# One loop over token groups: later layers in pieces between the heads, value and output weights fetched pair by pair

## The chip, the cores and the metric

The kernel runs on one core of one Trainium2 chip. The metric is device time in microseconds, the median of the runs shown. PE is TensorE (matrix products and transposes), DVE is VectorE, ACT is ScalarE, POOL is GpSimd, SP is SyncE, whose queue issues nearly all transfers.

## What is computed

4096 tokens (64 sequences of 64) of 256 features pass through four layers, each added to the tokens with a gate:

```python
x = x + jnp.tanh(g_xattn[0]) * _L0_xattn_ref(_layernorm(x), ctx_2048, ...)
x = x + jnp.tanh(g_ffn[0])   * _L0_ffn_ref(_layernorm(x), ...)
x = x + jnp.tanh(g_xattn[1]) * _L1_xattn_ref(_layernorm(x), ctx_2048, ctx_2048)
x = x + jnp.tanh(g_ffn[1])   * _L1_ffn_ref(_layernorm(x), ...)
```

- Layer 1: attention of each sequence's tokens to its context, 16 heads of 128; queries and keys are RMS-normalised over all 2048 inner features, then an output projection of 2048x256. (The text branch of the reference is empty here, since a context has 64 rows.)
- Layer 2: a dense 256x256 product with bias, plus a low-rank update by the two best of 8 experts, weighted by a softmax of their two logits.
- Layer 3: sigmoid attention per sequence, `V . sigmoid(Q^T K / 8)`, where the feature axes meet: a 256x256 affinity for each sequence.
- Layer 4: the best of 8 experts of rank 64, scaled by its probability.

## The kernel before

The tokens are worked on in 8 groups (`NG`) of 512, held as 4 tiles (`NT`) of 128. Matrix operands are split into a high and a low float32r part, and `three` computes hi.hi, hi.lo and lo.hi.

**Two programs, one after the other.** `first_attention` runs layer 1 for all groups and stores each group's result to memory (`x1_scratch`); `remaining_layers` then loads it and runs layers 2 to 4. The first holds the q, k, v and output weights, hi and lo, in SBUF; that memory is given to the second's tiles afterwards. Both use all 8 PSUM banks.

**First attention.** After a preparation (weights in, split in hi and lo, two Gram matrices that give the norms of queries and keys), each group takes 16 steps, one per head `h`. On each engine the order of a step is written out by hand in `step`. On PE: `prob_transpose(h-3)`, `output(h-4)`, the key projection of head h, `attend(h-3)`, `scores(h-1)`, `values(h)`, the query projection. On DVE: `prob_copy(h-3)`, `probabilities(h-2)`, `attn_lo(h-3)`, `logits(h-1)`. On ACT: the evacuation of keys, `attn_hi(h-3)`, values, `exps(h-1)`, queries. `scores` and `prob_transpose` share bank `at_ps`: PE may transpose head h-3 in step h only when DVE has taken the logits of head h-2 in step h-1; `attend(h-3)` needs `prob_copy(h-3)`; the next group's layer norm (`tile_stats`, `tile_variances`, `tile_scales`), its transposes and its Gram sums are spread over steps 2 to 14. In step 0 DVE also makes `ct_lo`, `xt_lo` (`split`) and the factors `rr` (`score_factors`).

**Remaining layers.** A software pipeline of three stages over groups: A (layer 2) of group i, B (layer 3) of i-1, C (layer 4) of i-2. `RING` lists in what order PE works and takes the 8 banks. A layer norm is `layernorm`: 4 `bn_stats` and 18 small operations, linked one by one. `low_parts` on POOL makes the low parts of the transposed tiles. `stay_awake` puts idle products of `w0t` on PE at the beginning and end of this pipeline. The output tile is stored group by group.

Of the kernel before, what the change touches and what calls it, by code (L numbers as in the profile page):

```python
# [5 lines left out]
F32 = mybir.dt.float32  # L18
F32R = mybir.dt.float32r
# [8 lines left out]
INNER = H * HD  # L28
DC = D // P
# [29 lines left out]

# [27 lines left out]

# [6 lines left out]
def rsqrt(dve, chain, y, t, v):  # L94
    rsqrt_guess(dve, chain, y, t, v)
    rsqrt_newton(dve, chain, y, t, v, 3)


def moments(dve, chain, mean, var_eps, t, stats):

# [6 lines left out]
    chain.link(dve.tensor_scalar(var_eps, t, 1.0 / D, LN_EPS, ALU.mult, ALU.add))  # L107

# [9 lines left out]
REST = "rest"  # L118


class Shared:
# [3 lines left out]
    def __init__(self, nc, stack):  # L125
        def sb(name, shape):
            return stack.enter_context(nc.sbuf_tensor(name, shape, F32))

        def sem(name):
            return stack.enter_context(nc.semaphore(name))  # L130

        self.ident = sb("ident", [P, P])
        self.tg = sb("tg", [P, 4])
        self.bias0 = sb("bias0", [P, D])
        self.gbias = sb("gbias", [P, E0])
        self.prefer = sb("prefer", [P, NT, E0])
        self.tokens = sb("tokens", [P, NT, D])
        self.context = sb("context", [P, NT, D])
        self.xs = sb("xs", [P, DC, GT])
        self.cs = sb("cs", [P, DC, GT])  # L140
        self.gram = sb("gram", [P, 2, DC, D + 1])
        self.gram_j = sb("gram_j", [P, 2, D])
        self.xres = sb("xres", [P, NT, D])
        self.s_raw = sem("s_raw_rest")
        self.rstd = sb("rstd", [P, NT])
        self.shift = sb("shift", [P, NT])
        self.scales = Signal(sem("scales_rest"), 1)
        self.x1_out = Signal(sem("x1_out"), 16)
        self.x1_in = Signal(sem("x1_in"), 16)
        self.cin_in = Signal(sem("cin_in_rest"), 16)  # L150


def raw_weights(shared):

    cs = shared.cs[:, :, :].rearrange("p c n -> p (c n)")
    return (cs[:, 0:DC * D].rearrange("p (c d) -> p c d", c=DC),
            cs[:, DC * D:DC * D + D],
            cs[:, DC * D + D:DC * D + 2 * D].rearrange("p (o e r) -> p o e r", o=2, e=E0),
            shared.xs[:, :, :].rearrange("p c n -> p (c n)").rearrange("p (c d) -> p c d", d=D),
            shared.gram[:, :, :, :].rearrange("p n c d -> p (n c d)")[:, 0:2 * E1 * R1].rearrange(  # L160
                "p (o e r) -> p o e r", o=2, e=E1),
            shared.gram_j[0:E0, :, :])


def first_attention(nc, shared, late, x, ctx, g_xattn, g_ffn, b0, gate_b,
                    q_w, q_b, ki_w, ki_b, vi_w, vi_b, o_w, o_b, nq_s, nki_s, x1_dram):


    CHAIN_PER = 100
    PREP_USES = 2 + 2 * 10  # L170
    PREP_BANKS = 6
    RAW_SLOTS = 3
    BSQ_READY = 2
    ATT_LAG, OUT_LAG = 3, 4
    LN_STEP, TR_STEP, GRAM_STEP = 6, 8, 9
    x_t = x.rearrange("b s d -> (b s) d").rearrange("(g t p) d -> g p t d", g=NG, p=P)
    c_t = ctx.rearrange("b s d -> (b s) d").rearrange("(g t p) d -> g p t d", g=NG, p=P)
    with ExitStack() as stack:
        def sb(name, shape, dt=F32):
            return stack.enter_context(nc.sbuf_tensor(name, shape, dt))  # L180

        def sem(name):
            return stack.enter_context(nc.semaphore(name))

        def signal(name, per):
            return Signal(sem(name), per)


        w_hi = {n: sb(f"{n}_hi", [P, DC, INNER], F32R) for n in "qkv"}
        w_lo = {n: sb(f"{n}_lo", [P, DC, INNER], F32R) for n in "qkv"}  # L190
        wo_hi = sb("wo_hi", [P, H, D], F32R)
        wo_lo = sb("wo_lo", [P, H, D], F32R)

        gram = shared.gram
        bsq = sb("bsq", [P, 2, H])
        beta = sb("beta", [P, 2])
        ident, xin, cin, xs, cs, xres, tg = (shared.ident, shared.tokens, shared.context, shared.xs, shared.cs,
                                             shared.xres, shared.tg)
        ones = sb("ones", [P, P])
# [1425 lines left out]
```

## Time and profile before

| | |
|---|---|
| Time, median of 3 runs (lowest to highest) | 1524.62 us (1524.61 to 1529.27) |
| Span of the profiled execution | 1542.4 us |
| PE busy | 1444.9 us, 94% |
| PE weight loads busy | 1272.6 us, 83% |
| DVE busy | 963.7 us, 62% |
| ACT busy | 639.9 us, 41% |
| POOL busy | 151.4 us, 10% |
| HBM traffic | 31.26 MB read, 8.39 MB written, 26 GB/s |

Busy times are those of one profiled execution, which took 17.8 us longer from first to last instruction than the median run. A matmul's end is modelled, so what PE really takes for a piece of work is read from the distance between starts.

### The profile page before, as it was taken

To read this page: it belongs to the slowest core of one execution; us is meant where nothing else is said; L and a number is where in the kernel's file an instruction comes from. 1 tells how busy PE (TensorE), PEld (TensorE's weight loads), DVE (VectorE), ACT (ScalarE), POOL (GpSimd) and SP (SyncE) were. 2 spreads that over 40 slices of the span, in tenths; PEclk is the share of its full clock that TensorE was granted. 3 is DMA by queue.
4 is the path that set the end of the run, shared out by engine and by line. 5 is a ranking of instruction groups with operands and counts; after the bars stand their busy time and mean duration, and the time that the engine had idled before them with its cause. 6 is when DMAs were issued, how large, how long until landed. Compare 5 with 4: busy or idle time off the path is not lost. (4 is left out here: it accounts for less than half of the span.)

```text
span 1542.4 us, 28883 instructions
## 1 busy us (share of the span) xinstructions
PE 1444.9 (94%) x10731; PEld 1272.6 (83%) x10731; DVE 963.7 (62%) x2915; ACT 639.9 (41%) x1125; POOL 151.4 (10%) x112
## 2 busy tenths in 40 slices
PE   6799999999999999999999999999778898889887
PEld 5689889989988988998898899888666777668766
DVE  6555665666576566657657666656667766685543
ACT  3334444344343443434434443444334344443442
POOL 3100000000000000000000000000112332232231
PEclk9999999999999999999999999999887887777787
DMA  5300000000000000000000000020000000100000
GB/s 181 114 2 1 29 28 2 28 2 28 16 15 28 1 29 28 1 28 2 28 1 29 28 1 1 25 73 1 28 28 28 29 28 27 41 27 14 27 15 28
DMA packets 32111, 41.30 MB, mean 27 GB/s; under 512 B 5473, under 2 KB 28993, under 8 KB 31361
## 3 DMA queue, kind: packets, MB, share of 16 engines
q1 hardware_dynamic: 31808, 39.38, 7.6%
q8 instruction: 91, 1.49, 0.4%
q0 software_dynamic: 192, 0.27, 0.1%
q14 instruction: 20, 0.16, 0.0%
HBM read 31.26 MB, written 8.39 MB: 26 GB/s over the span
## 5 line engine op out<-in xcount | busy, mean ns | idle before, releaser
L834 DVE SCALAR_TENSOR_TENSOR ao_lo<-bank,vecs,ao_hi 128x512 fp32r<-128x512 f32 x128 | 96.2, 751 | 227.7 <-ACT ao_hi L472 227.5
L827 DVE COPY pt<-bank 64x128 f32<-64x128 f32 x512 | 147.4, 288 | 127.3 <-PE bank L614 121.4
L483 ACT ACTIVATE k_sb<-bank,vecs 128x512 f32<-128x512 f32 x128 | 88.1, 688 | 260.7 <-PE bank L539 260.7
L487 ACT ACTIVATE v_sb<-bank 128x512 f32<-128x512 f32 x128 | 76.5, 598 | 233.4 <-PE bank L539 233.4
L539 PE MATMUL bank<-wo_hi,ao_hi 128*128 128x256 f32 x512 | 155.2, 303 | 2.7 <-DVE ao_lo L834 2.7
L539 PE MATMUL bank<-v_hi,ct_hi 128*128 128x256 f32 x512 | 156.3, 305 | 0.0
L539 PE MATMUL bank<-wo_hi,ao_lo 128*128 128x256 f32 x512 | 144.7, 283 | 0.0
L539 PE MATMUL bank<-wo_lo,ao_hi 128*128 128x256 f32 x512 | 144.6, 282 | 0.0
L539 PE MATMUL bank<-v_hi,ct_lo 128*128 128x256 f32 x512 | 144.4, 282 | 0.0
L539 PE MATMUL bank<-v_lo,ct_hi 128*128 128x256 f32 x512 | 144.3, 282 | 0.0
L623 PEld LDWEIGHTS bank<-pt,v_sb 128*128 128x128 f32 x1024 | 133.3, 191 | 13.2 <-issue 2.8
L623 PE MATMUL bank<-pt,v_sb 128*128 128x128 f32 x1024 | 136.8, 276 | 0.9 <-issue 0.4
L490 ACT ACTIVATE q_sb<-bank,qbias,qscale 128x512 f32<-128x512 f32 x128 | 99.5, 777 | 58.5 <-PE bank L539 58.5
L425 POOL TENSOR_TENSOR xres<-xres,obias 128x1024 f32<-128x1024 f32 x8 | 19.2, 2397 | 931.9 <-DMA xres<-in_x_dram 931.9
L472 ACT ACTIVATE ao_hi<-bank,vecs 128x512 fp32r<-128x512 f32 x128 | 87.9, 687 | 43.6 <-PE bank L623 43.6
L539 PE MATMUL bank<-ct_hi,k_hi 128*128 128x512 f32 x256 | 102.4, 400 | 3.0 <-DVE ct_lo L818 3.0
L1354 PE MATMUL ban2k<-context,xn 64*128 64x256 f32 x256 | 66.5, 552 | 41.2 <-DVE result L1536 33.3
L539 PEld LDWEIGHTS bank<-v_hi,ct_hi 128*128 128x128 f32 x512 | 96.6, 189 | 6.7 <-issue 0.2
L539 PE MATMUL bank<-xt_hi,q_hi 128*128 128x512 f32 x256 | 101.8, 398 | 0.0
L539 PE MATMUL bank<-xt_lo,q_hi 128*128 128x512 f32 x256 | 101.6, 397 | 0.0
L539 PE MATMUL bank<-ct_lo,k_hi 128*128 128x512 f32 x256 | 101.6, 397 | 0.0
L539 PE MATMUL bank<-xt_hi,q_lo 128*128 128x512 f32 x256 | 100.5, 392 | 0.0
(243 smaller groups left out, 3476.5 us busy)
## 6 DMA issues: line engine op xcount, KB each, us to landing
context<-in_ctx_dram SPq DMA_DIRECT2D x16, 512.0 KB, 4.8
tokens<-in_x_dram SPq DMA_DIRECT2D x8, 512.0 KB, 4.1
xres<-in_x_dram SPq DMA_DIRECT2D x8, 512.0 KB, 3.9
x_scratch<-xres SPq DMA_DIRECT2D x8, 512.0 KB, 2.6
tokens<-x_scratch SPq DMA_DIRECT2D x8, 512.0 KB, 3.3
out_dram<-result SPq DMA_DIRECT2D x8, 512.0 KB, 2.9
raw<-in_L_xattn_ki_w_dram SPq DMA_DIRECT2D x2, 1024.0 KB, 8.1
raw<-in_L_xattn_vi_w_dram SPq DMA_DIRECT2D x2, 1024.0 KB, 5.8
```

Source lines behind the costliest of these rows:

```text
L425: pool.tensor_tensor(xres[:, :, :], xres[:, :, :], obias[:, :].unsqueeze(1).to_broadcast([P, NT, D]), ALU.add).then_inc(xres_ready.sem, 1)
L472: act.activation(ao_hi[:, :], pv_ps[:, :], ACT.Identity, bias=vecs[:, 4 * H + h % H:4 * H + h % H + 1]).then_inc(ao_hi_ready.sem, 1)
L483: act.activation(k_sb[:, h % 2, :], bank[:, :], ACT.Identity, bias=vecs[:, 3 * H + h:3 * H + h + 1]).then_inc(pj_read.sem, 1)
L487: act.activation(v_sb[:, (h // 2) % 2, t:t + 2, :], bank[:, :].rearrange("p (t n) -> p t n", t=2), ACT.Copy).then_inc(pj_read.sem, 1)
L490: act.activation(q_sb[:, :], bank[:, :], ACT.Identity, scale=qscale[:, h:h + 1], bias=qbias[:, h:h + 1]).then_inc(pj_read.sem, 1)
L539: last = pe.matmul(out, lhs[a], rhs[b], start=start and n == 0, stop=stop and n == 2, **kw)
L623: last = pe.matmul(pv_ps[:, t * P:(t + 1) * P], v_sb[:, (h // 2) % 2, t, (h % 2) * HD:(h % 2 + 1) * HD], pt[:, t, :], start=True, stop=True)
L827: last = dve.tensor_copy(pt[b * SEQ:(b + 1) * SEQ, q::2, b * SEQ:(b + 1) * SEQ], src[:, :, b * SEQ:(b + 1) * SEQ])
L834: dve.scalar_tensor_tensor(out=ao_lo[:, :], in0=pv_ps[:, :], scalar=vecs[:, v:v + 1], in1=ao_hi[:, :].bitcast(F32), op0=ALU.add, op1=ALU.s ...
L1354: last = pe.matmul(b[:, c * D:(c + 1) * D], xn2[rows, t, c * P:(c + 1) * P], cin[rows, t, :], start=True, stop=True)
```

## The change

Both programs become one (`layers`). The loop body b works on layer 1 of group b and, between its heads, on layers 2 to 4 of group s = b-1 and on the preparation of group n = b+1. A step has five points, "a" to "e", at which the function `share` of each engine may place a piece: a is before the key projection, b after it, c before `values`, d after it, e after the query projection. I write (4,c) for step 4, point c. Body 0 has no later layers; body 8 (`NG`) has only them. Bodies 2 to 6 are a hardware loop.

```diff
+        def share(b, h, p):           # on ACT, cut
+            n, s, parts, at = b + 1, b - 1, parts_of(b), (h, p)
+            if "N" in parts:
+                if at == (1, "c"):
+                    normalise(n)
...
+            if "S" in parts:
+                if at == (4, "c"):
+                    later_normalise(s, 0, xres, xn1_ready)
+                if at == (4, "e"):
+                    turned(s, "xt1", 0, xt1_full, x2t[0], xt1_hi_ready)
+                if at == (8, "a"):
+                    later_normalise(s, 1, x2, xn2_ready)
+                if at == (11, "b"):
+                    later_normalise(s, 2, x2, xn3_ready)
...
-    w_hi = {n: sb(f"{n}_hi", [P, DC, INNER], F32R) for n in "qkv"}
+    w_hi = {n: sb(f"{n}_hi", [P, DC, INNER], F32R) for n in "qk"}
+    sv = sb("sv", [P, 2, 2, DC, 2 * HD], F32R)
+    so = sb("so", [P, 2, 2, 2, D], F32R)
...
+    o_ps, pj_ps, at_ps, pv_ps, side = banks[0:2], banks[2:4], banks[4], banks[5], banks[6:8]
...
+        def fetch_values(b, p, h):
+            sp.wait_ge(pj_full.sem, pj_full.count(b, 3 * h + 1))
+            sp.dma_start(pair(sv, p), v_dram[p]).then_inc(sv_in[p % 2].sem, 16)
...
+        def body(b):                  # on SP
+            if not is_body(b, NG - 1):
+                load_inputs(b + 1)
+            for h in range(1, H, 2):
+                fetch_outputs(b, (h - 1) // 2)
+                if h + 3 < H:
+                    fetch_values(b, (h + 3) // 2, h)
+                elif not is_body(b, NG - 1):
+                    if h == H - 1:
+                        store(b - 1)
+                    fetch_values(b, (h + 3 - H) // 2, h)
+                if h == 7:
+                    load_residual(b)
+                if h == 9:
+                    load_context(b)
...
-            pool.tensor_tensor(lo, feature_major(whole, j), hi.bitcast(F32), ALU.subtract).then_inc(ready.sem, 1)
+        def turned_low(s, name, j, hi_ready, ready):      # now on DVE
+            dve.tensor_tensor(lo, token_major(bank_of(name, j)), hi.bitcast(F32), ALU.subtract).then_inc(ready.sem, 1)
```

What moves and what changes, in full:

- **Pieces of the later layers** (S), by point: DVE statistics of x1 (3,d) to (4,a); normalised (4,c); turned (4,e), (5,a); expert rows `xa` (5,c), (5,d); choice (5,e); gates (6,b), (6,d); layer 2 product (7,a), (7,b); statistics (7,c) to (7,e); context turned (7,d), (7,e); normalised (8,a); context sum (8,b); 8 affinities (8,c) to (9,e); attention (10,a), (10,c); statistics (10,d) to (11,a); normalised (11,b); turned (11,d), (11,e); logits (12,b), (12,c); layer 4 from (12,e) to (15,b).
- **Pieces of the next group** (N): its statistics stand at (0,e), (1,a), (1,b) instead of steps 2 to 7, ACT's `normalise` at (1,c) instead of step 7, four transposes from (1,e) to (2,c) instead of steps 8 to 11, the Gram products from (2,d) to (3,b). Their count is unchanged.
- **PSUM**: all side pieces share two banks, `side`; the order of use is one list, and a piece waits until the bank's former content is read (`take`).
- **Weights**: values and outputs are split into hi and lo during body 0, one pair of heads per two steps, and kept in memory (`v_scratch`, `o_scratch`); from then on each pair (512 KB for values, 512 KB for outputs) is fetched anew in each body, into one of two buffers. Preparation waits for the q and k splits only. The small weights of layers 2 to 4 are loaded and turned in steps 12 to 15 of body 0.
- **POOL** keeps three operations of 128x1024 per body: the output bias, the bias of layer 2, the context sum. All low parts go to DVE, which reads the PSUM bank itself; ACT's float32 copies of the turned tiles fall away, except the context's.
- x1 stays in SBUF: no `x1_scratch`, no reload. `stay_awake` is gone.

In the hardware loop, on DVE, from the factors `rr` of step 0 to `ao_lo` of step 1. Before (`L811` `score_factors`, `L827` `prob_copy`, `L853` `probabilities`, `L834` `attn_lo`):

```order
L811 TENSOR_SCALAR rr<-bank,rqk 64x64 x8
L827 COPY pt<-bank 64x2x64 x4
L851 TENSOR_REDUCE rsum<-expo 128x4
...
L853 TENSOR_TENSOR prob<-expo,rinv 128x256
L834 SCALAR_TENSOR_TENSOR ao_lo<-bank,vecs,ao_hi 128x512
```

After:

```order
L1284 TENSOR_SCALAR rr<-bank,rqk 64x64 x8
...
L1242 BN_STATS stats<-xin 128x6 x4
L1299 COPY pt<-bank 64x2x64 x4
L1323 TENSOR_REDUCE rsum<-expo 128x4
...
L1325 TENSOR_TENSOR prob<-expo,rinv 128x256
L83 TENSOR_TENSOR mean<-stats 128x4
...
L89 TENSOR_SCALAR var_eps<-nt_t 128x4
...
L1251 SCALAR_TENSOR_TENSOR shift<-mean,rstd 128x4
L1306 SCALAR_TENSOR_TENSOR ao_lo<-bank,vecs,ao_hi 128x512
```

The four statistics now stand ahead of `prob_copy` of step 1, and the whole chain of the layer norm between `probabilities` and `attn_lo`.

On ACT, step 1 of the loop, where `xin` is normalised for the next group. Before (L483 keys, L472 `attn_hi`, L487 values, L477 exponentials):

```order
L483 ACTIVATE k_sb<-bank,vecs 128x512
...
L472 ACTIVATE ao_hi<-bank,vecs 128x512
...
L487 ACTIVATE v_sb<-bank 128x512
...
L477 ACTIVATE expo<-logit 128x256
...
L490 ACTIVATE q_sb<-bank,qbias,qscale 128x512
```

After:

```order
L644 ACTIVATE k_sb<-bank,vecs 128x512
...
L633 ACTIVATE ao_hi<-bank,vecs 128x512
...
L611 ACTIVATE xin<-xin,shift,rstd 128x256 x4
...
L648 ACTIVATE v_sb<-bank 128x512
...
L638 ACTIVATE expo<-logit 128x256
...
L651 ACTIVATE q_sb<-bank,qbias,qscale 128x512
L616 ISA
L618 ACTIVATE xs<-bank 128x2x128
```

The normalisation, which waits for DVE's `shift`, stands ahead of the evacuation of the values and of everything behind it.

## Rows read from the trace of the kernel before

**Rows 1.** The page: the clock granted to PE in 40 slices, in tenths.
```profile
PEclk9999999999999999999999999999887887777787
```
**Rows 2.** Stretches: from:to length, busy PE, PEld, DVE, ACT, POOL, clock, DMA.
```profile
57.11:1087.03 1029.92, 1024.17 (x8211) 914.56 (x8212) 643.80 (x1927) 434.00 (x733) 19.17 (x8) 1.00 0.06 19
1087.03:1104.47 17.44, 10.98 (x95) 9.84 (x93) 10.25 (x26) 3.26 (x5) 0.00 (x0) 1.00 0.00 1
1104.47:1542.40 437.93, 371.09 (x2200) 313.23 (x2200) 274.62 (x893) 179.83 (x363) 114.15 (x80) 0.81 0.08 28
```
**Rows 3.** The same columns: step 0 of a group, and a plain step.
```profile
445.59:453.81 8.22, 8.13 (x63) 7.00 (x64) 7.45 (x18) 3.98 (x6) 0.00 (x0) 1.00 0.01 4
461.37:468.93 7.56, 7.56 (x64) 6.80 (x63) 4.44 (x12) 3.09 (x5) 0.00 (x0) 1.00 0.01 2
```
**Rows 4.** DVE and PE in order of time in those two steps: start, length, line.
```profile
452.59 2.36 DVE L811 TENSOR_SCALAR rr<-bank,rqk 64x64 f32<-64x64 f32 x8
...
461.77 1.19 DVE L827 COPY pt<-bank 64x128 f32<-64x128 f32 x4 [1.12 <-PE bank L614]
...
463.66 0.42 DVE L853 TENSOR_TENSOR prob<-expo,rinv 128x256 f32<-128x256 f32 x1
...
464.40 1.05 PE L623 MATMUL bank<-pt,v_sb 128*128 128x128 f32 x8
...
466.21 0.75 DVE L834 SCALAR_TENSOR_TENSOR ao_lo<-bank,vecs,ao_hi 128x512 fp32r<-128x512 f32 x1 [2.12 <-ACT ao_hi L472]
...
467.78 0.42 DVE L845 TENSOR_TENSOR logit<-logit,rmax 128x256 f32<-128x256 f32 x1
```
**Rows 5.** Stretches of later layers, PE only: length, busy, clock, DMA.
```profile
1244.94:1268.64 23.70, 23.60 (x184) 1.00 0.12 41
1244.94:1247.67 2.73, 2.73 (x21) 1.00 0.44 156
1131.49:1133.15 1.66, 1.66 (x18) 1.00 0.00 0
1148.91:1150.95 2.04, 2.04 (x18) 1.00 0.00 0
1114.97:1115.42 0.45, 0.45 (x5) 1.00 0.00 0
```
**Rows 6.** Stretches on DVE: a layer norm, its end, a choice of experts.
```profile
22.81:27.60 4.79, 4.24 (x25) 1.00 0.76 284
25.66:27.60 1.94, 1.63 (x11) 1.00 1.05 443
1285.55:1288.24 2.69, 2.24 (x12) 0.50 0.00 0
```
**Rows 7.** A stretch on ACT: four tiles normalised.
```profile
1508.77:1510.89 2.12, 2.07 (x4) 1.00 0.02 4
```
**Rows 8.** POOL and DVE in order of time, where they meet.
```profile
615.97 2.39 POOL L425 TENSOR_TENSOR xres<-xres,obias 128x1024 f32<-128x1024 f32 x1 [129.84 <-DMA xres<-in_x_dram]
...
617.02 1.62 DVE L853 TENSOR_TENSOR prob<-expo,rinv 128x256 f32<-128x256 f32 x1
```
**Rows 9.** PE after two waits, and the clock behind the second (all engines).
```profile
1092.75 0.41 PE L614 MATMUL bank<-ident,prob 128*128 128x128 f32 x2 [2.28 <-DVE logit L845]
...
1276.83 2.73 PE L1354 MATMUL ban2k<-context,xn 64*128 64x256 f32 x8 [5.94 <-DVE result L1536]
...
1284.00:1288.00 4.00, 4.00 (x15) 3.04 (x15) 2.60 (x15) 1.01 (x3) 0.00 (x0) 0.50 0.00 0
```
**Rows 10.** The start of the first group's heads, DVE and PE.
```profile
52.28 2.29 DVE L316 TENSOR_TENSOR wo_lo<-raw,wo_hi 128x2048 fp32r<-128x2048 f32 x1
...
57.11 0.53 PE L539 MATMUL bank<-ct_hi,k_hi 128*128 128x512 f32 x1 [3.05 <-DVE ct_lo L818]
```
**Rows 11.** The last DVE operation, and a transfer: issues, size, us to landing.
```profile
1538.34 0.75 DVE L1536 SCALAR_TENSOR_TENSOR result<-ban2k,tg,result 128x512 f32<-128x512 f32 x1 [2.06 <-PE ban2k L1281]
...
tokens<-in_x_dram SPq DMA_DIRECT2D x8, 512.0 KB, 4.1
```

More of the change, by code:

```diff
@@ L107, in moments, with is_body @@
     chain.link(dve.tensor_scalar(var_eps, t, 1.0 / D, LN_EPS, ALU.mult, ALU.add))
+def is_body(b, n):
+    return isinstance(b, int) and b == n
 def identity(pool, sem, ident):
@@ L117 @@
 IDENT_READY = 2
[L118 to L150, printed above, removed]
@@ L165, in first_attention, with three @@
[L165 to L175, printed above, removed]
+BSQ_READY = 2
+PREP_USES = 2 + 2 * 10
+PREP_BANKS = 6
+ATT_LAG, OUT_LAG = 3, 4
+POINTS = "abcde"
+DVE_LOWS, POOL_LOWS = (0, 3), (1, 2)
+def three(pe, out, lhs, rhs, start, stop, **kw):
+    for n, (a, b) in enumerate(((0, 0), (0, 1), (1, 0))):
+        last = pe.matmul(out, lhs[a], rhs[b], start=start and n == 0, stop=stop and n == 2, **kw)
+    return last
@@ new lines, in layers @@
+    sv = sb("sv", [P, 2, 2, DC, 2 * HD], F32R)
+    so = sb("so", [P, 2, 2, 2, D], F32R)
+    xin = sb("xin", [P, NT, D])
+    cin = sb("cin", [P, NT, D])
+    xs = sb("xs", [P, DC, GT])
+    cs = sb("cs", [P, DC, GT])
+    xres = sb("xres", [P, NT, D])
+    stats = sb("stats", [P, NT, 6])
+    mean = sb("mean", [P, NT])
+    var_eps = sb("var_eps", [P, NT])
+    rstd = sb("rstd", [P, NT])
+    shift = sb("shift", [P, NT])
+    nt_t = sb("nt_t", [P, NT])
+    sums = sb("sums", [P, 2 * NT])
+    sums_b = sb("sums_b", [P, 2 * NT])
@@ new lines, in layers @@
+    rqk = sb("rqk", [P, 2 * NT])
+    nqk_t = sb("nqk_t", [P, 2 * NT])
+    rmax = sb("rmax", [P, NT])
+    rsum = sb("rsum", [P, NT])
+    rinv = sb("rinv", [P, NT])
+    with ExitStack() as early:
+        raw = [early.enter_context(nc.sbuf_tensor(f"raw{i}", [P, INNER], F32)) for i in range(4)]
+    xt_hi, xt_lo = both("xt", [P, DC, GT])
+    ct_hi, ct_lo = both("ct", [P, DC, GT])
+    v_sb = sb("v_sb", [P, 2, NT, 2 * HD])
+    k_sb = sb("k_sb", [P, 2, GT])
+    q_sb = sb("q_sb", [P, GT])
+    logit = sb("logit", [P, NT, SEQ])
@@ new lines, in layers @@
+    pick = [sb(f"pick{i}", [P, NT, E0]) for i in range(2)]
+    top = sb("top", [P, 2, NT])
+    best = sb("best", [P, NT])
+    gexp = sb("gexp", [P, NT])
+    gw = sb("gw", [P, 2, NT])
+    gates = sb("gates", [P, NT, E0])
+    csum = sb("csum", [P, NT])
+    lg1 = sb("lg1", [P, NT, E1])
+    ex1 = sb("ex1", [P, NT, E1])
+    coef = sb("coef", [P, NT, E1])
+    banks = [stack.enter_context(nc.psum_tensor(f"bank{i}", [P, 512], F32)) for i in range(8)]
+    o_ps, pj_ps, at_ps, pv_ps, side = banks[0:2], banks[2:4], banks[4], banks[5], banks[6:8]
@@ new lines, in layers, with parts_of, bank_of, token_major @@
+    PLACE = {(name, i): u for u, (name, i, _, _) in enumerate(SIDE)}
+    assert len(SIDE) % 2 == 0
+    GROUP = {"N": 1, "S": -1, "W": 0}
+    def parts_of(b):
+        if not isinstance(b, int) or 0 < b < NG - 1:
+            return "SN"
+        return {-1: "N", 0: "NW", NG - 1: "S", NG: "S"}.get(b, "")
+    def bank_of(name, i):
+        return side[PLACE[name, i] % 2]
+    def token_major(bank):
+        return bank[:, :].rearrange("p (t c n) -> p t c n", t=2, c=DC)
+    def feature_major(buf, i):
+        return buf[:, :, 2 * i * P:2 * (i + 1) * P].rearrange("p c (t n) -> p t c n", t=2)
```

2516 lines of the change are left out of this document (1274 added, 1242 removed).

## The prediction

> **What bounds the kernel now.** I read the page's clock line first: PE has its full clock for three quarters of the span and less in the last quarter [rows 1]. The stretches say why [rows 2]. From the first head's first product to the last group's last one, 1029.9 us, PE is busy for 1024.2 at clock 1.00, and no wait of weight stands there: PE is the bound and everything else hides behind it. Then 17.4 us of drain (the last heads' outputs), then 437.9 us for the later layers, with PE busy for 371.1 at a mean clock of 0.81. That last stretch is what the change is about. Its waits are serial chains: layer norm on DVE, normalising on ACT, transposing on PE. A wait of 2.28 us left the next products at full speed, but after one of 5.94 us PE ran at 0.50, its 1.2 GHz level, and was still there 7 us later, busy without a break [rows 9]. So the later layers pay twice, by idling and by the clock after it.
>
> Next, a plain step of one head. It takes 7.56 us, all of it PE, while DVE is busy for 4.4 and ACT for 3.1 [rows 3]. That leaves room on DVE for side work, but the order matters. In the plain step [rows 4] `prob_copy` runs from 0.4 to 1.6 and `attend` starts at 3.05, so the copy may be 1.4 us late. The last operation of the logits ends at 6.8 and the next step starts at 7.56, so it may be 0.7 us late, plus what PE does for side pieces behind `scores`. Step 0 has more on DVE: 8.22 us long [rows 3], and DVE's `rr` ends 9.4 us after the step began [rows 4], which the next step still absorbs.
>
> **The later layers on PE, at full clock.** A stretch of 23.70 us without a real gap holds three of the four expert tiles `h`, half of the gate logits, `xg`, the layer 2 product, `hm`, `att`, `y` and 16 transposes [rows 5]. The missing tile with the missing half of the logits is the row of 2.73. Eight more transposes are half of 1.66. The affinities are twice 2.04 (16 of 32 records each). `xa` has 24 products; four starts lie in 0.45, so 2.7. Sum 34.0 per group. Cut into some 34 pieces, each first product follows another kind; the rows do not price that alone. I bound it by 0.5 us (the long stretch holds seven kinds and shows 0.1 us idle) and 11 us (step 0, in which two pieces stand in another order, is 0.66 us longer than a plain one [rows 3]) and take 2, near the low end, since the stretch is PE work of the very kinds that move and step 0 also waits for the splits. So **36 us** per group that must go between the heads. It hides nothing on PE: PE was full, and stays full. What the change can save is the idling and the slow clock: 437.9 us become 8 x 36 = 288 at most, less what comes back as waits.
>
> **What comes back as waits in a body.** DVE's side work is about 36 us per group too: three layer norms of 4.79 [rows 6], choices and gates about 8, some sixteen 128x512 operations at 0.7 (with the eight low parts that leave POOL), the context sum. Against it stand 36 us more PE time and 16 steps x 3.1 us of free DVE. On average it fits; locally it does not. I walked the body step by step with the row values:
> - Step 1: DVE is free at 9.4. The statistics (2.85 for statistics and variances [rows 6], half of it here) bring it to 10.8, the copy to 12.0, while PE wants `attend` at 8.2 + 3.05 = 11.3. PE waits **0.8**. Then `probabilities` to 13.1, variances and scales (1.4 + 1.94) to 16.5, and ACT's `normalise` 2.1 [rows 7] to 18.6. PE stands at (1,e) from 16.6 and waits **2.0** for the first transpose. Queued behind `normalise` on ACT are the values' evacuation, the exponentials and the queries; PE needs them later than 18.6, so no more is added.
> - Step 4: after the two residuals of step 3, DVE does 2.85 at (3,d), (3,e) and enters step 4 3.4 us late; copy to 4.7, `attend` wanted at 3.05: **1.6**. Scales and ACT's normalising end at 9.9, PE is at (4,e) from 9.2: **0.6**.
> - Step 5: `square_norms` and the low part of `xt1` stand ahead of the copy: **1.4**. Step 6, behind the choice of 2.69 [rows 6]: **0.3**.
> - Step 8: the whole layer norm (7,c) to (7,e), 4.79, starts when the logits of step 7 are done: **1.3**. Queued behind it are the copy and, on ACT, the keys' evacuation behind `later_normalise` (8,a).
> - Steps 11 and 12: on ACT the normalising at (11,b) stands ahead of `attn_hi`; the transposes wait **1.2**, the next step **0.3** for the logits.
> - Steps 9, 10, 13 to 15: PE has 3 to 5 us of side work each and DVE at most 2: nothing.
>
> Sum **9.5 us** per body for bodies 1 to 6, some 5 for body 7, which prepares no next group.
>
> **Moved at no price.** ACT loses six copies per group and stays under half busy. The next group's transposes and Gram products are the same. Each body fetches 16 transfers of 512 KB for the weights and five others, some 10.7 MB in all in 165 to 180 us; one lands in 4.1 us [rows 11], while each has two to three steps, 15 us or more, between the wait that frees its buffer and its use. SP's queue is in order: `load_residual` stands behind `fetch_values` of step 7 and so starts only after that step's `values`; it has until POOL's bias, and that until the next body. If this cover were gone, each late fetch would cost its lateness in full; I see none.
>
> **Preparation.** The first product waits for DVE, which made `wo_lo` (2.29) in between [rows 10]; that goes to body 0. What is late next are the Gram sums, which now pass through one bank at a time. I take 1.4 us, between 0 and 3. Body 0 pays the 2.0 at (1,e), 28 transposes of late weights at 0.1 and a little: 6.
>
> **The end.** Body 8 has no heads to hide behind, and no second group to overlap: 17.4 drain; three layer norms with normalising 3 x 6.9 = 20.7; PE's 34 us, partly at 1.2 GHz after long waits [rows 9], 48; hi and low parts 5; choices and gates 7; residuals 2; 4 for waits on the two banks; from the last DVE operation to the end 3.3 [rows 11]. Sum **108**, between 100 and 118.
>
> **Sum.** Start 55.7, heads 1029.9, later layers 7 x 36 = 252, waits 6 x 9.5 + 5 = 62, body 0 6, end 108: **1514 us** of span against 1542.4, so 28 less. The median run stands 17.8 below the profiled span; the same difference off 1524.6 gives **1497**. I predict 1498.
>
> **POOL, and a rule on it.** POOL's bias ran from 615.97 to 618.36; `prob`, which starts at 617.02 and reads two SBUF tiles, took 1.62 instead of 0.42 and ended 0.3 after POOL [rows 8]. So DVE stands still for such operations. Three of them per body, 6.7 us. In my walk the one at 51 to 54 us falls where DVE would wait for ACT anyway and costs 1.2 (counted in step 5); the output bias lands just behind the layer norm of step 7; the third falls where there is slack. The Trainium skill, page "SBUF — State Buffer", section "Who interferes with whom", says more: whichever engine starts first holds the shared ports for its whole instruction and the other blocks fully, and copies and scalar operations in a two-port mode are hit too. By that the small operations of `square_norms` and of the layer norm would all be stopped. The row agrees for two SBUF inputs; no row here shows the scalar ones, so the sum goes by the walk.
>
> **Rivals.**
> 1. *Forecast* (50%): waits of 7 to 12 us per body: 1482 to 1514.
> 2. *More hides than I see* (12%): DVE and ACT run ahead in steps 9 to 15 and the late steps recover; waits of 2 to 6: 7 x 5 less, 1460 to 1482.
> 3. *DVE falls behind, slower* (22%): the residual load lands early or late, POOL's bias meets the layer norm of (7,c) to (7,e), 2.4 us more in front of `prob_copy`, and the other two POOL operations cost 1.5 each instead of 1.2 and 0; each piece cut off by a wait on another engine costs 0.1 more. With 4 to 8 us more per body it decides: break-even lies at 28 / 7 = 4 us more. Price: 1525 to 1550. For it: every wait in the walk is DVE's; the walk has no reserve for handovers. Against: before, step 0 took up 2.4 us of `rr` and the splits at 0.66 us of PE's time. This is where the page's rule would put it: 6.7 us of lost DVE, 5.5 more than counted, give 1498 + 7 x 5.5 = 1536.
> 4. *The clock falls in each body* (8%): my longest wait is 2.0 us, and 2.28 did no harm [rows 9]; but two waits close together might. Work of some 16 us at half clock costs 8: 7 x 8 more, 1554.
> 5. *No net change* (8%): between 1 and 3, 1514 to 1530.
>
> The overlap itself cannot fail to happen; the order on PE is written out. Faster by over 0.3% (a measurement of this kernel can't tell less from no change) is below 1520: cases 1 and 2 and part of 5, 66%. Within 0.3%: 8%. Slower: 26%. Leaving out the top of case 2 and the ends of 3 and 4, the range is 1470 to 1545.
>
> **What would show it.** Profile after: clock 1.00 until the last body; bodies of 175 us (distance between POOL's output biases), 165 with rival 2, 180 with 3; waits on PE before `attend` on `prob_copy`'s DVE line at steps 1, 4, 5, 8 and before `transposes` on ACT's `xin`; PE waits of some 62 us before the end; from the last query product to the end 108. Wrong would be: waits on DMA, a clock below 1.00 inside the bodies, or waits in steps 9, 10 or 13 to 15.

## The result and the profile after

The changed kernel takes **1546.22 us** (1544.57 to 1554.43, 6 runs) against 1530.20 (1524.61 to 1535.20, 6 runs) for the kernel before beside it: ratio 1.0104, interval 1.0067 to 1.0141, so slower by 1.0%. I had forecast 1498, and the range to 1545 ends just below it.

The page of the kernel after:

```profile
span 1542.8 us, 28633 instructions
PE 1419.3 (92%) x10671; PEld 1224.8 (79%) x10671; DVE 976.3 (63%) x3000; ACT 599.5 (39%) x1065; POOL 63.8 (4%) x42
PEclk9999999999999999999999999999999999999858
HBM read 85.78 MB, written 12.58 MB: 64 GB/s over the span
```

The overlap does what it was made for: PE's clock line is full until the last three slices, where before it fell in the last quarter [rows 1], and PE is busy for 26 us less. Yet the span is the same, 1542.8 against 1542.4. To see where the gain went I cut the span at POOL's output bias, which comes once per body (start, length):

```profile
635.20 2.35 POOL L556 TENSOR_TENSOR xres<-xres,obias 128x1024 f32<-128x1024 f32 x1 [34.48 <-DMA xres<-in_x_dram]
...
815.76 2.35 POOL L556 TENSOR_TENSOR xres<-xres,obias 128x1024 f32<-128x1024 f32 x1 [34.64 <-DMA xres<-in_x_dram]
```

The stretches between, and the whole of the heads and of the end (from:to, length, then busy time and count of PE, PE's weight loads, DVE, ACT, POOL, the granted clock, the DMA share, GB/s):

```profile
635.20:815.76 180.56, 171.39 (x1306) 147.58 (x1306) 117.47 (x368) 72.30 (x130) 6.62 (x3) 0.99 0.18 62
815.76:997.24 181.48, 171.42 (x1306) 147.66 (x1306) 117.70 (x369) 72.22 (x130) 6.63 (x4) 0.99 0.18 62
...
49.31:1434.43 1385.12, 1317.34 (x10089) 1137.57 (x10089) 901.71 (x2786) 561.80 (x1003) 48.91 (x22) 0.99 0.19 65
1434.43:1542.80 108.37, 64.74 (x358) 53.67 (x356) 44.15 (x148) 21.59 (x40) 4.24 (x2) 0.73 0.02 5
```

The end takes 108.4 us; I had forecast 108. A body takes 181; I had forecast 175. In the first stretch shown PE is not busy for 180.56 - 171.39 = 9.2 us; I had forecast 9.5 of waits. So the sum of the waits was right, and PE's *busy* time is some 6 us too long. PE's waits in that body (total, times, longest) and some of them in order of time, in brackets the idle time ahead and its releaser:

```profile
PE bank L897 <- DVE pt L1299: 4.9, 4, 1.5
PE bank L961 <- ACT xn L657: 1.5, 2, 1.1
PE bank L888 <- issue: 0.9, 1, 0.9
PE bank L908 <- issue: 0.8, 1, 0.8
PE bank L864 <- ACT xin L611: 0.7, 1, 0.7
```

```profile
593.23 1.16 PE L897 MATMUL bank<-pt,v_sb 128*128 128x128 f32 x8 [1.49 <-DVE pt L1299]
...
603.73 1.16 PE L897 MATMUL bank<-pt,v_sb 128*128 128x128 f32 x8 [1.24 <-DVE pt L1299]
...
636.42 1.16 PE L897 MATMUL bank<-pt,v_sb 128*128 128x128 f32 x8 [1.34 <-DVE pt L1299]
...
676.90 0.66 PE L961 MATMUL bank<-ident,xn 128*128 128x128 f32 x4 [1.14 <-ACT xn L657]
```

These are `attend` of steps 4, 5 and 8 and the turning at (11,d): 1.49, 1.24, 1.34 and 1.14 where the walk had 1.6, 1.4, 1.3 and 1.2. Three things were not in the walk.

**The affinities.** PE in order of time in step 8, one affinity and the product behind it:

```profile
638.12 1.13 PE L999 MATMUL bank<-cin,xn 64*128 64x256 f32 x4
639.18 0.50 PE L116 MATMUL bank<-sv,ct_hi 128*128 128x256 f32 x2
```

The next product starts 1.06 after it, and so behind the others. Eight such pieces are 8.5 us. Before, 16 records (four affinities) lay in 2.04, so eight in 4.1 [rows 5]. An affinity uses 64 of PE's 128 rows; before, one sequence's product could stand beside the next one's on the other rows, and now each has a piece for itself.

**The clock.** PE in body 2, the first pass of the hardware loop, with the two waits of step 1, and stretches behind them:

```profile
377.14 1.16 PE L897 MATMUL bank<-pt,v_sb 128*128 128x128 f32 x8 [0.99 <-DVE pt L1299]
...
383.84 0.41 PE L864 MATMUL bank<-ident,xin 128*128 128x128 f32 x2 [1.92 <-ACT xin L611]
```

```profile
382.00:384.00 2.00, 0.16 (x2) 0.19 (x3) 1.43 (x4) 2.00 (x6) 0.00 (x0) 1.00 0.56 223
384.00:386.00 2.00, 2.00 (x13) 2.00 (x13) 1.03 (x4) 1.57 (x5) 0.00 (x0) 0.59 0.04 8
386.00:388.00 2.00, 2.00 (x12) 2.00 (x12) 1.14 (x4) 0.00 (x0) 0.00 (x0) 0.56 0.00 0
388.00:390.00 2.00, 2.00 (x14) 1.69 (x14) 0.00 (x0) 1.13 (x3) 0.00 (x0) 1.00 0.00 0
```

Both waits have the forecast size (0.8 and 2.0), but behind them PE runs at its 1.2 GHz level for 3.4 us, which loses 1.7. A single wait of 2.28 had done no harm [rows 9]. Each of bodies 2 to 6 has one such stretch. Body 1 has none, although its waits in step 1 are nearly the same and as close together (for the second the profile names no releaser here):

```profile
199.11 1.16 PE L897 MATMUL bank<-pt,v_sb 128*128 128x128 f32 x8 [1.18 <-DVE pt L1299]
...
205.65 0.41 PE L864 MATMUL bank<-ident,xin 128*128 128x128 f32 x2 [1.74 <-issue]
```

```profile
206.00:208.00 2.00, 2.00 (x20) 2.00 (x19) 1.40 (x5) 1.54 (x5) 0.00 (x0) 1.00 0.00 0
```

**Waits without a releaser.** In step 0 of bodies 3 to 6, that is each time behind a jump back of the hardware loop, PE stands twice for nothing that the profile shows, 1.8 to 2.8 us in sum. Bodies 1, 2 and 7, which no jump back precedes, have no such gaps. In body 5:

```profile
907.55 0.43 PE L888 MATMUL bank<-ident,prob 128*128 128x128 f32 x2 [0.88 <-issue]
...
913.52 0.70 PE L908 MATMUL bank<-k_sb,q_sb 128*64 128x64 f32 x8 [1.95 <-issue]
```

### The profile page after: what moved, and what is told of

The parts are those of the page before. It is cut to its first block, busy times and chain, and to the rows that moved or that the text cites. A ratio compares the mean times of both kernels' runs of the same rounds, so it can differ in the third digit from the quotient of the medians.

```text
span 1542.8 us, 28633 instructions
## 1 busy us (share of the span) xinstructions
PE 1419.3 (92%) x10671; PEld 1224.8 (79%) x10671; DVE 976.3 (63%) x3000; ACT 599.5 (39%) x1065; POOL 63.8 (4%) x42
## 4 chain that ended last, share of the span: by engine, by line
PE 67%; DVE 21%; issue 6%; ACT 4%; DMA 0%; SPq 0%; DVEq 0%; ACTq 0%
PE bank L116 44%; PE bank L897 7%; PE bank L999 4%; PE bank L908 3%; PE bank L874 3%; DVE pt L1299 3%; DVE stats L1341 2%; PE bank L888 2%; ACT ao_hi L633 2%; ACT xn L657 1%; DVE rmax L1316 1%; PE bank L1011 1%; PE bank L864 1%; DVE logit L1314 1%; DVE ao_lo L1306 1%
## 5 line engine op out<-in xcount | busy, mean ns | idle before, releaser
L116 PE MATMUL bank<-so,ao_hi 128*128 128x256 f32 x1024 | 198.0, 292 | 2.9 <-DVE ao_lo L1306 2.9
L116 PE MATMUL bank<-sv,ct_hi 128*128 128x256 f32 x1024 | 197.8, 292 | 0.0
L897 PEld LDWEIGHTS bank<-pt,v_sb 128*128 128x128 f32 x1024 | 127.3, 191 | 52.3 <-DVE pt L1299 41.6
L116 PEld LDWEIGHTS bank<-sv,ct_hi 128*128 128x128 f32 x1024 | 156.2, 189 | 12.8 <-issue 7.8
L116 PEld LDWEIGHTS bank<-so,ao_hi 128*128 128x128 f32 x1024 | 156.5, 190 | 3.3 <-issue 3.3
L116 PE MATMUL bank<-so,ao_lo 128*128 128x256 f32 x512 | 143.6, 280 | 0.0
L116 PE MATMUL bank<-sv,ct_lo 128*128 128x256 f32 x512 | 142.9, 279 | 0.0
L116 PE MATMUL bank<-ct_hi,k_lo 128*128 128x512 f32 x256 | 102.9, 402 | 0.0
L116 PEld LDWEIGHTS bank<-so,ao_lo 128*128 128x128 f32 x512 | 96.8, 189 | 0.0
L116 PEld LDWEIGHTS bank<-sv,ct_lo 128*128 128x128 f32 x512 | 96.3, 188 | 0.0
```

Source lines behind the costliest of these rows:

```text
L116: last = pe.matmul(out, lhs[a], rhs[b], start=start and n == 0, stop=stop and n == 2, **kw)
L897: last = pe.matmul(pv_ps[:, t * P:(t + 1) * P], v_sb[:, (h // 2) % 2, t, (h % 2) * HD:(h % 2 + 1) * HD], pt[:, t, :], start=True, stop=True)
```

## The experiments

Times are medians of 4 or 5 runs (10 in the repeat of the kernel before); ratios are to the kernel before on the same chip, 1530 to 1534 us. Experiments 1 to 4 ran on one chip, 5 to 7 on a second, 8 and 9 on a third and 10 on a fourth, so a difference between two of these sets is good to a few us only.

**1. Affinities in pairs.** The changed kernel with

```diff
-            for c in range(DC):
-                last = pe.matmul(dst[:, c * D:(c + 1) * D], xn[rows, t, ...], cin2[rows, t, :], ...)
-            last.then_inc(aff_full.sem, 1)
+            for c in range(DC):
+                for i in range(2):
+                    rows = slice(i * SEQ, (i + 1) * SEQ)
+                    last = pe.matmul(dst[i][:, c * D:(c + 1) * D], xn[rows, t, ...], cin2[rows, t, :], ...)
+    PAIR_AT = {(8, "c"): 0, (8, "e"): 1, (9, "b"): 2, (9, "d"): 3}
```

> The changed kernel with one edit: the eight affinities of a group are issued as four pairs, each pair with the two sequences of one tile (rows 0 to 63 and 64 to 127), product by product in turn into the two side banks, at (8,c), (8,e), (9,b) and (9,d). Theory A (the affinities were priced from a stretch where two of them ran at the same time on the two halves of PE's rows; cut into single pieces they no longer overlap): each pair takes 1.0 to 1.1 us instead of 2 x 1.06, PE's affinity time per body falls from 8.5 to about 4.2, bodies from 181 to 177, and the whole from 1546 to about 1515. Theory B (the bodies are long because of DVE, of the waits it causes, or of the cuts as such): PE's saved time turns into waits on prob_copy, bodies stay at 180 or lose at most the four cuts, 1 us, and the time stays above 1538.

1519.64 us, ratio 0.9919 (0.9889 to 0.9948): 27 us less than the changed kernel. PE's piece in the trace, now two affinities:

```profile
635.24 1.13 PE L1001 MATMUL bank<-cin,xn 64*128 64x256 f32 x8
```

Twice the records in the same 1.13. Theory A's size was 31 less. Two things gave part of it back. One is POOL (experiment 5). The other is the end: from the last query product it takes 112.9 us instead of 108.8, and there each pair behind the first waits for ACT, which empties the banks:

```profile
1470.44 2.08 PE L1001 MATMUL bank<-cin,xn 64*128 64x256 f32 x8 [1.23 <-ACT th L682]
```

**2. The control.** The same with `rows = slice(0, SEQ)` for both.

> Control for the run with pairs: the same four pairs at the same places, but both products of a pair read rows 0 to 63, so the odd sequences get the affinity of the even ones (that part of the output is not the reference's). Theory A (overlap on different rows): a pair takes 2.0 us or more, as two single ones, and the time stays within 5 us of the changed kernel, 1538 to 1546. Rival (what the pairs save is four cuts between kinds of products): this run is as fast as the pairs, about 1515.

1544.49 us, 1.0088 (1.0063 to 1.0112), the time of the changed kernel. A pair now takes 1.99:

```profile
643.96 1.99 PE L1001 MATMUL bank<-cin,xn 64*128 64x256 f32 x8
```

So it is the two halves of the rows that give the gain, and not the four cuts fewer: the next product starts 1.92 behind such a pair, against 2 x 1.06 for two single pieces. The Trainium skill, page "TensorEngine Tiling (Array Packing)", section "Tiling Modes", says that tiles of the array can load weights and multiply in parallel; these rows agree.

**3. PE's loop written out.** The changed kernel with `for b in range(2, NG - 1)` in place of PE's hardware loop.

> The changed kernel with one edit: PE's hardware loop over bodies 2 to 6 is written out; the other engines keep theirs. In the trace PE idles in step 0 of each pass for nothing that is recorded (0.94 before the transposes, 0.84 to 1.9 in the middle of scores), and PE then runs some 3.4 us at its 1.2 GHz level. Theory C (the jump back of PE's loop costs this): these gaps go, 2.3 us per pass, and with them the slow stretch, 1.7 us per pass; 5 passes, so 1546 becomes 1526 to 1538. Rival (the gaps are waits on another engine or on the splits of the tokens): they stay, and the time with them.

1549.72 us, 1.0154 (1.0106 to 1.0201): nothing gained. But the gaps moved. PE's two are gone, and in the same bodies 3 to 6 DVE has one (in body 5, DVE, then PE):

```profile
907.21 1.20 DVE L1299 COPY pt<-bank 64x128 f32<-64x128 f32 x4 [4.01 <-issue]
...
908.46 1.90 PE L897 MATMUL bank<-pt,v_sb 128*128 128x128 f32 x8 [1.91 <-DVE pt L1299]
```

PE's transposes for this copy started at 904.75, 2.5 before it; in the changed kernel the copy starts 1.2 behind them. So DVE was 1.3 late on its own account, behind the jump of its own loop. Theory C's forecast failed; its mechanism may be incomplete rather than wrong: experiments 6 and 10 go on from here.

**4. Fetches made small.** The changed kernel with `pair(sv, p)[:, 0:16]` and `v_dram[p][:, 0:16]`, the same for the outputs. The index cuts columns, not partitions as I wrote: each fetch moves 16 columns of all 128 partitions, 8 KB.

> The changed kernel, but each fetch of a pair of value or output weights moves 16 of 128 partition rows (64 KB instead of 512 KB); nearly all heads then use stale weights, so the output is not the reference's. Theory D (the transfers are hidden, as forecast): within 3 us of the changed kernel. Rival (10 MB per body of writes into SBUF slow the engines' own accesses or delay instruction loading): bodies of 181 become 178 or less, time below 1530.

1571.20 us, 1.0262 (1.0236 to 1.0287): *slower* by 25 us than the changed kernel, as neither theory had it. The residual lands 3.8 us from its issue instead of 5.0 (the page's issues), behind smaller transfers in SP's queue, and so POOL's output bias starts sooner, in six of seven bodies inside the layer norm of (7,c) to (7,e). In the worst of them, POOL and DVE in order of time, PE's next wait, and the clock behind it:

```profile
1005.80 2.35 POOL L556 TENSOR_TENSOR xres<-xres,obias 128x1024 f32<-128x1024 f32 x1 [33.57 <-DMA xres<-in_x_dram]
1005.82 2.35 DVE L77 TENSOR_TENSOR ntmp<-rstd 128x4 f32<-128x4 f32 x1
1008.20 0.16 DVE L78 SCALAR_TENSOR_TENSOR ntmp<-ntmp,var_eps 128x4 f32<-128x4 f32 x1
...
1010.13 2.07 PE L897 MATMUL bank<-pt,v_sb 128*128 128x128 f32 x8 [3.53 <-DVE pt L1299]
```

```profile
1010.00:1015.00 5.00, 4.87 (x28) 3.88 (x28) 4.39 (x10) 2.12 (x4) 1.89 (x1) 0.50 0.00 0
1015.00:1020.00 5.00, 5.00 (x17) 3.80 (x16) 0.00 (x0) 1.19 (x2) 0.00 (x0) 0.50 0.00 0
```

An operation on 128x4 takes 2.35 instead of 0.16, just as long as POOL's; `attend` waits 3.5 instead of 1.3; and PE then runs at 1.2 GHz for over 10 us. That is rival 3's meeting and rival 4's clock, one setting off the other. In the changed kernel the bias starts behind the layer norm in all seven bodies, but by less than a microsecond; at 815.76 it is 0.35 us behind the end of the last operation:

```profile
815.25 0.16 DVE L1350 SCALAR_TENSOR_TENSOR shift<-mean,rstd 128x4 f32<-128x4 f32 x1
```

It escapes by luck.

**5. POOL's operations moved, and made small.** Both on top of the pairs. In the pairs run the gain of PE had moved the bias into the layer norm in four of seven bodies:

```profile
625.95 2.34 POOL L557 TENSOR_TENSOR xres<-xres,obias 128x1024 f32<-128x1024 f32 x1 [34.13 <-DMA xres<-in_x_dram]
626.02 2.29 DVE L1353 SCALAR_TENSOR_TENSOR shift<-mean,rstd 128x4 f32<-128x4 f32 x1
...
629.47 1.16 PE L898 MATMUL bank<-pt,v_sb 128*128 128x128 f32 x8 [3.26 <-DVE pt L1302]
```

```diff
+            pool.wait_ge(l_ready.sem, l_ready.count(b, 8))      # output bias, now behind the context sum
+            pool.wait_ge(l_ready.sem, l_ready.count(s + 1, 5))  # bias of layer 2
+            pool.wait_ge(l_ready.sem, l_ready.count(s + 1, 7))  # context sum
```

> The kernel with paired affinities (1519.6 us), with POOL's three operations moved: each also waits until DVE has finished the logits of a certain step (bias of layer 2: step 6, context sum: step 8, output bias: step 9, behind the context sum), so that it starts where DVE would idle. In the pairs run POOL's output bias started inside the layer norm of (7,c) to (7,e) in four of seven bodies: an operation of 128x4 that takes 0.16 took 2.3, and attend waited 3.2 instead of 1.1 to 1.3. Theory E (POOL's operation stops DVE's): attend of step 8 waits 1.3 in every body, 4 x 2 us less and a little at steps 5 and 9: 1505 to 1513. Rival (the waits come from the order on DVE itself): within 3 us of 1519.6.

1507.01 us, 0.9852 (0.9795 to 0.9908). The second kernel, on one column per tile:

> The kernel with paired affinities, with POOL's three operations per body cut to one column of each tile (128x4 instead of 128x1024): the output bias, the bias of layer 2 and the context sum are left out of all other columns. Theory E: the full price of POOL beside DVE, 4 x 2 us for the met layer norms and up to 1 us in other places of each body: 1502 to 1512, and the kernel with timed POOL operations not slower than this by more than 4 us. Rival: within 3 us of 1519.6.

1505.33 us, 0.9837 (0.9780 to 0.9895). POOL's meetings with DVE cost some 13 us in the pairs kernel, and a wait of POOL's for the right moment gives all but 2 of it back. The body between the biases is 174.83 long here, at clock 1.00. The Trainium skill, page "SBUF — State Buffer", section "Who interferes with whom", says that a DVE instruction with two SBUF inputs contends with a GpSimd instruction that reads SBUF, and that whichever issues first keeps the shared ports for its whole instruction while the other blocks fully; the rows of 2.35 and 2.29 agree. That side of the rule I had left out of the sum.

**6. All loops written out**, on top of the pairs, POOL not yet timed.

> The kernel with paired affinities (1519.6 us), with the hardware loops of all five engines written out. With PE's loop alone written out, PE's two unrecorded gaps of step 0 went, but DVE then stood for 4.0 us ahead of prob_copy for nothing that is recorded, and attend waited 1.9 for it; bodies kept their length. Theory C2 (each engine pays about 1 us at its own jump back, and they stand in line): with all loops written out both kinds of gap go, some 3 us per pass and the slow clock behind them, 5 passes: 1500 to 1507. Rival (something else in step 0 holds PE, such as the splits): the waits return under another name and the time stays at 1515 to 1523.

1510.79 us, 0.9846 (0.9780 to 0.9912); the median lies between C2's range (1500 to 1507) and the rival's (1515 to 1523), and the four runs between 1500 and 1514, too wide to tell C2's size. PE's gaps without a releaser in step 0 are gone, and so is DVE's: `attend` of step 0 starts without a wait.

**7. DVE retimed, at the wrong places.** On top of the timed POOL:

```diff
-                if at == (4, "d"):
+                if at == (9, "c"):
                     square_norms(n)
-                if at == (5, "b"):
+                if at == (9, "e"):
                     norm_factors()
-                if at == (3, "e"):
+                if at == (4, "a"):
                     later_variances()
```

and the turning of `xt3` from (11,d), (11,e) to (11,e), (12,a) on PE, ACT and DVE.

> The kernel with paired affinities and timed POOL operations, with three moves on DVE besides: square_norms and norm_factors from (4,d), (5,b) to (9,c), (9,e); the variances of the first later layer norm from (3,e) to (4,a); and the turning of xt3 one point later on all engines, (11,e) and (12,a). Theory F (the waits of attend at steps 4 and 5, 1.5 and 1.2 us, and of the transposes at (11,d), 1.1 us, are DVE work standing ahead of prob_copy or of the scales): each goes to under 0.4, some 3 us per body, 7 x 3 = 21: 1486 to 1496. Rival (DVE has no slack there, the work only moves the wait to the next step's transposes): 1500 to 1512.

1512.07 us, 0.9872 (0.9817 to 0.9928): 5 *more* than without. Theory F falls in this form. ACT and PE in order of time around step 11:

```profile
657.45 2.08 ACT L664 ACTIVATE xn<-x,shift,rstd 128x256 f32<-128x256 f32 x4 [1.43 <-DVE shift L1359]
...
662.19 0.44 PE L895 MATMUL bank<-ident,prob 128*128 128x128 f32 x2 [1.95 <-DVE logit L1326]
```

The waits of steps 4, 5 and 11 went, but ACT's normalising still stood ahead of `attn_hi`, so that `attn_lo`, the logits and the transposes of step 12 were late by what had been hidden under the old wait; `later_variances` behind the copy only moved 1.5 us to (4,e), where the transposes now waited 1.8; and `square_norms` at (9,c) met the output bias (2.58 for two operations of 128x4). The clock fell twice per body. A wait that is taken away uncovers the next one in the same chain.

**8. DVE's work moved into idle time.** Timed POOL, all loops written out, and instead of those moves:

```diff
                     residual(s, "lora", 0, lora_full, tg[:, 2:3], xres, x2_ready)
+                    dve.wait_ge(x2_ready.sem, x2_ready.count(s, 0))
+                    later_stats(x2, (0, 1))
...
+                if at == (3, "a"):
+                    first_residual(s, 0)
+                    dve.wait_ge(x1_ready.sem, x1_ready.count(s, 0))
+                    later_stats(xres, (0, 1))
+                if at == (3, "b"):
+                    first_residual(s, 1)
```

with `square_norms` at (9,a) and `norm_factors` at (14,e).

> Paired affinities, timed POOL operations (these two together 1507.0 us) and all hardware loops written out, and on DVE: the statistics of two tiles taken behind the first of the two residuals instead of all four behind the second, in step 7 and in step 3 (there both residuals move to (3,a) and (3,b), into idle time of 1.6 and 0.7 us); square_norms to (9,a) and norm_factors to (14,e). Theory H (waits fall when the work moves into DVE's idle time rather than behind another chain): attend's waits of 1.3 to 1.5 at steps 4, 5 and 8 go to under 0.3 each, 4 us per body; the loops give another 1 to 2 per pass as they did beside the pairs: 1470 to 1482. Rival (as in the retimed kernel, each wait comes back one step on): 1495 to 1505.

1466.33 us, 0.9559 (0.9513 to 0.9606): 4 us better than the low end of theory H. Of the 41 us below the kernel with timed POOL, 14 are the loops' if they cost here what they cost in experiment 10, and 27 are then left for DVE's moves, 4 per body as forecast. In the next step ACT and PE follow:

```diff
-                if at == (11, "b"):
+                if at == (11, "c"):
                     later_normalise(s, 2, x2, xn3_ready)
-                if at == (1, "e"):
+                if at == (2, "a"):
                     transposes(b, 0)
```

and `xt3` turned at (11,e), (12,a).

> The same, and the third layer norm's normalising on ACT from (11,b) to (11,c), behind attn_hi, with the turning of xt3 at (11,e) and (12,a); the next group's first transposes from (1,e) to (2,a), together with the second. Theory H: the waits of 1.1 at (11,d) and 1.9 at (1,e) go, up to 3 us per body, and with the one at (1,e) the slow clock behind it: 1450 to 1468. Rival (the retimed kernel's new waits were not ACT's order): a wait of about 1.9 before the probabilities' transposes of step 12 as there, and no gain over the kernel with split statistics.

1453.05 us, 0.9468 (0.9422 to 0.9513): 5.3% faster than the kernel before. One body between the biases, and all that PE waits for in it:

```profile
617.73:784.29 166.56, 163.61 (x1310) 143.96 (x1306) 114.62 (x367) 71.97 (x129) 6.68 (x4) 1.00 0.20 67
```

```profile
PE bank L894 <- DVE logit L1324: 1.7, 1, 1.7
PE bank L903 <- DVE pt L1306: 1.2, 1, 1.2
```

Both are left in steps 1 and 2, behind the next group's layer norm. The wait that I feared for step 12 didn't come: with the normalising behind `attn_hi` there is none.

**9. The kernel before, once more.**

> The kernel before, unchanged, profiled once more. My forecast took the profiled execution of before (1542.4 us of span, 17.8 above the median run) for a constant difference between a profiled span and a timed run. In the changed kernel the time stood 1.7 above the span in every run. Theory G (the span of the kernel before varies with the clock of its later layers, and the profile on record was a long one): this profile's span again lies 1.5 to 2 below its own run's time, that time is between 1523 and 1541, and the difference to 1542.4 lies behind 1087 us, in the later layers. Rival (profiling itself adds 18 us to this kernel): the span is 1540 or more while the timed runs are at 1530.

1532.51 us (1527.14 to 1538.55), ratio to itself 0.9988 (0.9962 to 1.0014). The profiled execution took 1531.84 with a span of 1530.0. Its last stretch, beside that of the profile on record:

```profile
1104.50:1530.00 425.50, 359.80 (x2197) 302.89 (x2195) 273.81 (x892) 178.62 (x362) 113.24 (x80) 0.83 0.08 28
```

```profile
1104.50:1542.40 437.90, 371.09 (x2200) 313.23 (x2200) 274.62 (x893) 179.83 (x363) 114.15 (x80) 0.81 0.08 28
```

All of the 12.4 us lies in the later layers, and 11.3 of it is PE's busy time at another mean clock. Theory G holds: the span lies 1.8 below its own run's time, and the span of this kernel varies with its clock. The spans of all its runs beside the experiments lie between 1521.7 and 1539.6, so that the 1542.4 on record was a long execution even so; its own time is not known.

**10. The loops back.** The 1453 us kernel with all five hardware loops.

> The fastest kernel (1453.05 us, all loops written out) with the hardware loops of all five engines back, nothing else changed. Theory C2 (a jump back costs PE two gaps that are not recorded, of about 1 us each, in step 0 of each pass, and the 1.2 GHz level behind them): bodies 2 to 6 and the one behind the loop grow by 1 to 3 us each, 1459 to 1469. Rival (in this kernel DVE and ACT have room to take the gaps up, and PE's gaps fall where it would wait anyway, in step 1): 1453 to 1457.

1467.07 us, 0.9583 (0.9559 to 0.9606), 14.0 more, inside theory C2's range. But it lies otherwise than C2 had it, over six bodies. From one output bias to the next:

```profile
452.05 2.38 POOL L559 TENSOR_TENSOR xres<-xres,obias 128x1024 f32<-128x1024 f32 x1 [8.74 <-DVE logit L1324]
...
621.23 2.39 POOL L559 TENSOR_TENSOR xres<-xres,obias 128x1024 f32<-128x1024 f32 x1 [8.72 <-DVE logit L1324]
```

The way into the loop (body 1 to 2) takes 166.6 and the way out (body 6 to 7) 156.2, as without loops (166.5 and 156.5). The four distances with a jump back in them are 169.2, 171.3, 170.5 and 169.0 instead of 166.5 to 166.6. So five passes have four jumps back, and each costs 2.5 to 4.7 us, 3.5 in the mean. PE behind one of them:

```profile
690.39 0.43 PE L894 MATMUL bank<-ident,prob 128*128 128x128 f32 x2 [0.90 <-issue]
...
697.00 1.01 PE L914 MATMUL bank<-k_sb,q_sb 128*64 128x64 f32 x14 [2.21 <-issue]
```

The Trainium skill, page "Runtime: NRT & Kernel Launch", section "Instruction fetch mechanics", says that a taken branch whose target is not already in the prefetched pages stalls until that target is fetched. The runs show where such time would lie and what it costs; they don't show the fetch itself.

## Why the prediction was wrong

Where the 48 us between 1498 and 1546 are:

| term | forecast | measured |
|---|---|---|
| start (first product) | 55.7 | 49.3 |
| first product to last query product | 1350 | 1385.1 |
| of it, one body | 175 | 181 |
| of it, PE's waits in a body | 9.5 | 9.2 |
| of these, gaps behind a jump back (bodies 3 to 6) | 0 | 1.8 to 2.8 |
| of it, the 8 affinities | 4.1 | 8.5 |
| of it, lost to the clock in a body | 0 | 1.7 |
| end | 108 | 108.4 |
| span | 1514 | 1542.8 |
| time minus span | -17.8 | +1.8 |

- **The step that turned the sign** is the term "The affinities are twice 2.04". Count and row were right, but the row was of products that run side by side on the two halves of PE's rows, and the change puts each into a piece of its own: 8.5 us per body instead of 4.1, 4.4 more, 31 in seven bodies. Experiments 1 and 2 show it and undo it. That alone turned faster into slower: with pairs the kernel is at 1519.6, 0.8% faster than the kernel before.
- **The second** is the conversion at the end of the sum: "The median run stands 17.8 below the profiled span; the same difference off 1524.6 gives 1497". The difference was no property of profiling but one long execution of the kernel before (experiment 9). In the changed kernel, which spends little time at a varying clock, the time is the span plus 1.8. It is 19 of the 48 us (16 between 1514 and 1498, and 3.4 between the span and the median after). A span of 1514 meant a time of about 1516, against a kernel before of 1530. This step moved the number but not the direction.
- **The third** is the clock. "My longest wait is 2.0 us, and 2.28 did no harm" reads one wait by itself. Waits of 1.0 and 1.9 between 376 and 384 us, or of 0.9, 0.8 and 0.8 in step 0 of body 4, were enough for 3.4 us at 1.2 GHz, while 1.2 and 1.7 in body 1 were not. I had it as a rival at 8%, priced at 8 us per body where it costs 1.7, 8.5 us in five bodies. No experiment takes this term away by itself; it is read from the rows.
- **The fourth** is what stands at nothing in the walk: the gaps behind a jump back, 9 us in four bodies. Experiment 10 shows what such gaps cost in the fastest kernel.
- **The walk of waits was right** step by step: 1.5 for 1.6 at step 4, 1.24 for 1.4, 1.34 for 1.3, 1.14 for 1.2, 1.9 for 2.0 at (1,e) of body 2, 0.4 for 0.6 at (4,e); the two of 0.3 (steps 6 and 12) did not come. In bodies 3 to 6 the wait at (1,e) was 0.66, since step 0's two gaps, which I had not, gave DVE and ACT time. The sum of 9.5 met 9.2 partly by that exchange, which is luck.
- **PE's work otherwise** was right: the pieces of the later layers sum to 37.8 by their distances, with pairs to 37.8 - 4.2 = 33.6, for 34.0. The 2 us for switches were needed, but not in these pieces: the heads' own products and the next group's pieces take 134.1 in a body of the changed kernel, 132.4 without the 1.7 lost to the clock, for 129.7 before (the distance from one group's `rr` to the next's, 322.86 to 452.59). In the fastest kernel they take 130.5, and 129.7 + 33.6 + 2.9 of waits = 166.2, measured 166.6. Why they are 2 us longer in the changed kernel stays open.
- **Transfers** were hidden, as forecast: PE waits on no fetch in any body. But they were not without effect. They set when POOL starts, and experiment 4 got slower by taking them away.
- **Rival 3** gave the time (1525 to 1550) by a mechanism that was not at work in the changed kernel: there the bias just misses the layer norm. It was at work in the kernels of experiments 1 (four bodies of seven) and 4 (six of seven), at 2 us per meeting, as priced. That the time fell into this rival's range is chance. POOL was not idle in the changed kernel, though: in body 3 its bias of layer 2 (598.33 to 600.72) stops `square_norms`, whose operation takes 2.28 where the next ones take 0.17. It is a TENSOR_SCALAR, one of the operations for which the prediction had no row:

```profile
598.47 2.28 DVE L1268 TENSOR_SCALAR sums_b<-sums_b 128x8 f32<-128x8 f32 x1
```

  The walk had 1.2 for this meeting in step 5.
- **Start and end**: the first product came 7.8 us sooner than before, where I had taken 1.4; I did not look into why. The end was 0.4 longer. Its affinities too were priced side by side, and I did not take it apart, so that the hit shows none of its terms to be right.

What stays open: which combination of waits brings the clock down (each case here is told by its rows, none by a rule), and why PE's second gap behind a jump back varies between 0.3 and 2.5.

## What to carry to other kernels

Price a piece of work from a row in which it stands in the neighbourhood that it will have after the change: products on half of PE's rows cost half only beside a partner. When a profiled span and the timed runs differ, find the stretch that differs before using the difference. And where a body is full, first look at what other engines do at the same moment (POOL beside DVE, the jump of a loop), then move work into idle time that the trace shows, not just behind the operation that was late. And when a loop's cost is to be found, compare the way in, the jumps back and the way out one by one.

## What the hardware showed that I had not expected

- An operation of 128x4 on DVE that takes 0.16 us stood for 2.35, the whole of POOL's operation of 128x1024; so did a TENSOR_SCALAR of 128x8, for 2.28.
- Two affinities (products of 64 rows) on different halves of PE's rows took 1.13 together, and 1.99 on the same half.
- A jump back of a hardware loop of this size costs 2.5 to 4.7 us against the same code written out, in gaps on PE (or on DVE, when PE's loop alone is written out) and in the clock behind them. The way in and the way out cost nothing.
- Two waits of 1.0 and 1.9 us were followed by 3.4 us at 1.2 GHz in body 2, and two of 1.2 and 1.7 in body 1 by none.
- Less traffic (28 MB read instead of 86) made the kernel 25 us slower; the rows show POOL starting sooner, inside DVE's layer norm.
